# Cross-attention and a Fourier product on one core: a row left out of the first transform, 16-bit turning, a halved last product, one mask product

## What is computed

```python
x = x + xattn(layernorm(x), ctx, mask, wq, bq, wk, bk, wv, bv, wo, bo)   # x: 2 x 2048 x 512, ctx: 2 x 128 x 512
x = x + ffn(layernorm(x), w_freq_real, w_freq_imag, bias)

def xattn(...):   # 16 heads of 32
    score = einsum(q, k) / sqrt(32) * mask
    score = where(score == 0, -1e9, score)
    return softmax(score) @ v  @ wo + bo

def ffn(x, w_freq_real, w_freq_imag, bias):
    return real(ifft(fft(x) @ complex(w_freq_real, w_freq_imag))) + bias
```

## Time and profile before

| | |
|---|---|
| median of 3 runs | 470.81 (470.68 to 471.02) |
| the profiled execution's own time | 470.67 |
| its span, first to last instruction | 468.9 |
| granted TensorE clock, mean | 0.996 of full |
| TensorE busy | 449.5 (96%) |
| VectorE busy | 413.7 (88%) |
| ScalarE busy | 375.8 (80%) |
| GpSimd busy | 374.7 (80%) |
| chain that ended last | TensorE 70%, VectorE 12%, issue 7%, DMA 3%, GpSimd 3% |

### The profile page before, as it was taken

The page is one execution under the profiler, slowest core; times in us unless marked ns, Lnnn a source line. Parts: engine busy times, 40 slices in busy tenths (PEclk is TensorE's granted clock), DMA queues, the critical chain, the costliest instruction groups (busy, mean ns, idle before and its releaser), DMA issues.

```text
span 468.9 us, 11312 instructions
## 1 busy us (share of the span) xinstructions
PE 449.5 (96%) x3538; PEld 297.9 (64%) x3538; DVE 413.7 (88%) x698; ACT 375.8 (80%) x1431; POOL 374.7 (80%) x519
## 2 busy tenths in 40 slices
PE   7989979898999999999999999999999999999997
PEld 5877656676566666666666666666666666555443
DVE  4797499999999999999999999999999998999452
ACT  3358766789998989898989898988888898989620
POOL 6689666895998989898989898998989784866662
PEclk9999998999999999999999999999999999999999
DMA  8996834132435453644545554435332523331243
GB/s 291 396 358 166 263 137 112 42 86 69 93 82 133 114 141 107 141 120 125 136 114 146 100 121 117 108 105 143 105 95 62 98 75 80 78 92 25 67 112 113
DMA packets 83308, 59.37 MB, mean 127 GB/s; under 512 B 39729, under 2 KB 70705, under 8 KB 82738
## 3 DMA queue, kind: packets, MB, share of 16 engines
q1 hardware_dynamic: 82816, 58.55, 45.1%
q10 hardware_dynamic: 434, 0.10, 0.1%
HBM read 29.27 MB, written 8.39 MB: 80 GB/s over the span
## 4 chain that ended last, share of the span: by engine, by line
PE 70%; DVE 12%; issue 7%; DMA 3%; POOL 3%; SPq 2%; ACT 2%; DVEq 0%; POOLq 0%
PE bank L398 30%; PE bank L470 14%; PE bank L524 8%; PE bank L541 6%; PE bank L512 4%; DVE zs L786 3%; PE bank L537 2%; PE bank L403 2%; SPq L260 2%; DVE nmin L798 2%; DMA cxs<-in_ctx 1%; DMA xs<-in_x 1%; DVE zs L793 1%; PE bank L473 1%; ACT zs L626 1%
## 5 line engine op out<-in xcount | busy, mean ns | idle before, releaser
L626 ACT ACTIVATE zs<-zs,nbias 128x128 f32<-128x128 f32 x512 | 199.5, 397 | 5.4 <-POOL nbias L1018 5.2
L626 ACT ACTIVATION_READ_ACCUMULATOR zs<-zs,nbias 128x1 f32 x512 | 99.1, 194 | 0.0
L793 DVE SCALAR_TENSOR_TENSOR zs<-zs 128x1024 f32<-128x1024 f32 x64 | 92.0, 1437 | 2.3
L786 DVE TENSOR_TENSOR zs<-bank,ms 128x512 f32<-128x512 f32 x128 | 82.1, 683 | 0.0
L798 DVE TENSOR_REDUCE nmin<-zs 128x8 f32<-128x1024 f32 x64 | 77.2, 1206 | 0.1
L635 ACT COPY pt<-bank 128x512 f32<-128x512 f32 x128 | 68.5, 587 | 10.2 <-PE bank L524 9.7
L470 PE MATMUL bank<-xth,wqh 128*128 128x256 f16 x256 | 70.9, 277 | 2.2 <-DVE kl L745 1.8
L470 PE MATMUL bank<-xth,wql 128*128 128x256 f16 x256 | 70.4, 275 | 0.0
L470 PE MATMUL bank<-xtl,wqh 128*128 128x256 f16 x256 | 70.4, 275 | 0.0
L524 PE MATMUL bank<-ident,zs 128*128 128x128 f32 x512 | 67.0, 274 | 0.4 <-ACT zs L626 0.4
L1024 POOL COPY rzb<-rz 128x256 f32<-128x256 f32 x64 | 60.9, 951 | 3.1 <-DVE rz L803 2.2
(11 more groups left out here) (109 smaller groups left out, 983.9 us busy)
## 6 DMA issues: line engine op xcount, KB each, us to landing
xs<-in_x SPq DMA_DIRECT2D x16, 512.0 KB, 4.2
xtr<-in_xt SPq DMA_DIRECT2D x16, 512.0 KB, 4.7
out<-x SPq DMA_DIRECT2D x32, 256.0 KB, 2.3
qs<-qh SPq DMA_DIRECT2D x120, 64.0 KB, 2.0
lp<-in_lparts SPq DMA_DIRECT2D x4, 1024.0 KB, 9.2
qs<-ql SPq DMA_DIRECT2D x60, 64.0 KB, 2.0
ms<-in_mask SPq DMA_DIRECT2D x16, 128.0 KB, 2.3
wqs<-in_wq SPq DMA_DIRECT2D x2, 512.0 KB, 6.7
```

What stands on the lines that cost most here:

```text
L626: last = act.activation(z, z, ACT.Exp, bias=nbias[:, s % 4, i:i + 1], scale=-NEG, accum_out=zsum[:, s % 4, i:i + 1])
L786: dve.tensor_tensor(zs[:, s % NZ, t], A[n % 2][:].rearrange("p (h k) -> p h k", h=4), ms[:, c % NM, t, :].unsqueeze(1).broadcast_to([128, ...
L793: dve.scalar_tensor_tensor(out=z, in0=z, scalar=0.0, in1=z, op0=ALU.is_equal, op1=ALU.subtract).then_inc(eq_done, 1)
```

## The change

1. **Row of frequency 0.** In the host's table it is 0 in place of 0.5 for the first transform, so no mean has to be taken off: the statistics, their combination and the subtraction go from the four `U` fills. The second transform needs the 0.5: GpSimd writes it into the table in slot 8, once TensorE has done the last `U` fill, and the `M` fills wait for that.
2. **16-bit turning.** `stok` is float16, ScalarE makes a float16 copy of the identity in the head, and the turning is a plain float16 product against it.
3. **Halved last product.** The last `FF` fill becomes two, of columns 0 to 255 and 256 to 511, each with its own VectorE instruction and its own store.
4. **One mask product.** The two score banks are one tensor; a step has one mask product of 128x1024. It waits for both tiles' scores, and the next step's scores wait for all of it.

```diff
@@
+        if mid == [LAST]:
+            mid = [LAST, (*LAST, "right")]
@@
-        stok, _ = sb("stok", [128, 2, 2, 128], F32)
+        stok, _ = sb("stok", [128, 2, 2, 128], F16)
+        ident16, _ = sb("ident16", [128, 128], F16)
@@
-        bank = [stack.enter_context(nc.psum_tensor(f"bank{i}", [128, 512], F32)) for i in range(8)]
-        A, PB, CX, G = bank[0:2], bank[2:4], bank[4], bank[5:8]
+        A = stack.enter_context(nc.psum_tensor("scores", [128, 2, 512], F32))
+        bank = [stack.enter_context(nc.psum_tensor(f"bank{i}", [128, 512], F32)) for i in range(2, 8)]
+        PB, CX, G = bank[0:2], bank[2], bank[3:6]
@@
+
+        def columns(n):
+
+            if fills[n] == LAST:
+                return slice(0, 256)
+            return slice(256, 512) if fills[n][:3] == LAST else slice(0, 512)
@@
             def load_mask(c):
...
-                    sp.wait_ge(tt_done, 2 * (4 * (c - NM) + 3) + 2)
+                    sp.wait_ge(tt_done, 4 * (c - NM) + 4)
@@
             def store(c, t):
...
-                sp.wait_ge(g_free, at["FF", c, t] + 1)
-                sp.dma_start(o_d[:, n], x1[:, n % NO, :]).then_inc(d_o[n % NO], 16)
+                for f in fills:
+                    if f[:3] == ("FF", c, t):
+                        n1 = columns(at[f])
+                        sp.wait_ge(g_free, at[f] + 1)
+                        sp.dma_start(o_d[:, n, n1], x1[:, n % NO, n1]).then_inc(d_o[n % NO], 16)
@@
             def stat_rows(o, c):
...
+                if c == 0:
+                    pe.wait_ge(i16_done, 1)
...
-                    last = pe.transpose(o[:, 256 + 128 * t:384 + 128 * t], stok[:, c % 2, t], ident[:])
+                    last = pe.matmul(o[:, 256 + 128 * t:384 + 128 * t], stok[:, c % 2, t], ident16[:], start=True, stop=True)
@@
                 elif kind == "M":
...
+                    pe.wait_ge(dc_done, 1)
@@
-                    last = split_mm(o[:], [((h[:, f, k, :], l[:, f, k, :]), (mh[:, k, :], ml[:, k, :]))
-                                           for k in range(4)])
+                    n1 = columns(n)
+                    last = split_mm(o[:, n1], [((h[:, f, k, :], l[:, f, k, :]), (mh[:, k, n1], ml[:, k, n1]))
+                                               for k in range(4)])
...
             def scores(s, t):
...
-                if n >= 2:
-                    pe.wait_ge(tt_done, n - 1)
+                if t == 0 and s >= 1:
+                    pe.wait_ge(tt_done, s)
...
-                        last = full_mm(A[n % 2][:, 128 * j:128 * j + 128],
+                        last = full_mm(A[:, n % 2, 128 * j:128 * j + 128],
@@
+            act.wait_ge(d_eye, 16)
+            act.copy(ident16[:], ident[:]).then_inc(i16_done, 1)
@@
                 elif kind == "U":
...
-                    dve.bn_stats(stu[:], src[:, 0:256]).then_inc(u_done, 1)
-                    dve.wait_ge(u_done, 2 * c + 1)
-                    dve.bn_aggr(agu[:], stu[:]).then_inc(u_done, 1)
-                    dve.wait_ge(u_done, 2 * c + 2)
...
-                        last = dve.scalar_tensor_tensor(out=us[:, c, 256 * i:256 * i + 256], in0=src[:, 0:256],
-                                                        scalar=agu[:, 0:1], in1=od[:, c % 2], op0=ALU.subtract, op1=o)
+                        last = dve.tensor_tensor(us[:, c, 256 * i:256 * i + 256], src[:, 0:256], od[:, c % 2], o)
@@
                 elif kind == "FF":
...
-                    last = dve.scalar_tensor_tensor(out=x1[:, n1 % NO, :], in0=src[:], scalar=rs2[:, n1 % NO:n1 % NO + 1],
-                                                    in1=x1[:, n1 % NO, :], op0=ALU.mult, op1=ALU.add)
+                    z = x1[:, n1 % NO, columns(n)]
+                    last = dve.scalar_tensor_tensor(out=z, in0=src[:, columns(n)], scalar=rs2[:, n1 % NO:n1 % NO + 1],
+                                                    in1=z, op0=ALU.mult, op1=ALU.add)
@@
-            def mask_mul(s, t):
-                n = 2 * s + t
+            def mask_mul(s):
...
-                dve.wait_ge(sc_done, n + 1)
+                dve.wait_ge(sc_done, 2 * s + 2)
...
-                if t == 0 and s >= NZ:
+                if s >= NZ:
...
-                dve.tensor_tensor(zs[:, s % NZ, t], A[n % 2][:].rearrange("p (h k) -> p h k", h=4),
-                                  ms[:, c % NM, t, :].unsqueeze(1).broadcast_to([128, 4, KEYS]),
+                dve.tensor_tensor(zs[:, s % NZ], A[:].rearrange("p t (h k) -> p t h k", h=4),
+                                  ms[:, c % NM].unsqueeze(2).broadcast_to([128, 2, 4, KEYS]),
...
             def zero_to_neg(s):
...
-                dve.wait_ge(tt_done, 2 * s + 2)
+                dve.wait_ge(tt_done, s + 1)
@@
+
+            def constant_row():
+
+                pool.wait_ge(g_done, at["U", 3] + 1)
+                pool.memset(tb[0:1, 0, :], 0.5).then_inc(dc_done, 1)
@@
             for v in range(V0, V1):
...
+                if v == 8:
+                    constant_row()
@@
-    c[0] = 0.5
+    c[0] = 0.0```

On VectorE, slot 4 and the opening of slot 5 (`us` are the U fill's sums, `lp` the folding of the weights, `zs` the softmax tile, `nmin` its minimum). Before:

```order
L798 TENSOR_REDUCE nmin<-zs 128x8
L759 TENSOR_TENSOR ql<-bank,qh 128x256
L730 BN_STATS stu<-bank 128x6
L732 BN_AGGR agu<-stu 128x2
L735 SCALAR_TENSOR_TENSOR us<-bank,agu,od 128x256 x2
L823 BN_STATS st_91<-xs 128x6
L803 RECIPROCAL rz<-zsum 128x8
L828 BN_AGGR ag_92<-st_91 128x2
L841 TENSOR_TENSOR lp<-lp 128x512 x3
L786 TENSOR_TENSOR zs<-bank,ms 128x512 x2
L793 SCALAR_TENSOR_TENSOR zs<-zs 128x1024
```

More of the change, by code:

```diff
@@ L20 @@
 V0, V1 = 2, NS + 16
+LAST = ("FF", NC - 1, 1)
 NEG = 1e9
@@ L182, in build @@
         rs2, _ = sb("rs2", [128, NO], F32)
-        stu, _ = sb("stu", [128, 6], F32)
-        agu, _ = sb("agu", [128, 2], F32)
         nmin, _ = sb("nmin", [128, 4, 8], F32)
@@ L229, in build @@
         g_hi, ex_done, pt_copied, ch_done = (sem(n) for n in ("g_hi", "ex_done", "pt_copied", "ch_done"))
-        w_hi, w_sc, rc_done = sem("w_hi"), sem("w_sc"), sem("rc_done")
+        w_hi, w_sc, rc_done, i16_done = sem("w_hi"), sem("w_sc"), sem("rc_done"), sem("i16_done")
         h1_done, h2_done, st_done, wz_hi = (sem(n) for n in ("h1_done", "h2_done", "st_done", "wz_hi"))
@@ L235, in build @@
             sem(n) for n in ("rz_done", "cn_done", "s1_done", "a1_done", "s2_done", "a2_done", "w_lo"))
-        u_done, wz_lo, l0_done, m_hi, m_lo, b_zero, l2_done, l_hi, o_lo = (sem(n) for n in ("u_done", "wz_lo", "l0_done", "m_hi", "m_lo", "b_zero", "l2_done", "l_hi", "o_lo"))
+        dc_done, wz_lo, l0_done, m_hi, m_lo, b_zero, l2_done, l_hi, o_lo = (sem(n) for n in ("dc_done", "wz_lo", "l0_done", "m_hi", "m_lo", "b_zero", "l2_done", "l_hi", "o_lo"))
         p_l1, p_l2, p_zero = (sem(n) for n in ("p_l1", "p_l2", "p_zero"))
@@ L387, in _ @@
             for i in range(NO):
-                sp.wait_ge(d_o[i], 16 * len(range(i, 2 * NC, NO)))
+                sp.wait_ge(d_o[i], 16 * (len(range(i, 2 * NC, NO)) + (i == NO - 1)))
         @block.tensor
@@ L511, in scores @@
                 for j in range(4):
-                    last = pe.matmul(A[n % 2][:, 128 * j:128 * j + 128], qs[c % 2][0:96, g, j, 128 * t:128 * t + 128],
+                    last = pe.matmul(A[:, n % 2, 128 * j:128 * j + 128], qs[c % 2][0:96, g, j, 128 * t:128 * t + 128],
                                      ks[0:96, g, j, c // (NC // NB), :], start=True, stop=True)
@@ L892, in _ @@
             low_q(1)
-            mask_mul(0, 0)
-            mask_mul(0, 1)
+            mask_mul(0)
             lo(at["W1", 1])
@@ L899, in _ @@
             moments(2)
-            mask_mul(1, 0)
-            mask_mul(1, 1)
+            mask_mul(1)
             zero_to_neg(1)
@@ L916, in _ @@
                 if 0 <= v < NS:
-                    mask_mul(v, 0)
-                    mask_mul(v, 1)
+                    mask_mul(v)
                 if 0 <= v < NS:
@@ L1183, in dft_tables @@
     c, s = np.cos(2 * np.pi * kj / D), np.sin(2 * np.pi * kj / D)
-    c[0] = 0.5
+    c[0] = 0.0
     s[0] = 1.0 - 2.0 * (np.arange(n) % 2)
```

## The result

The changed kernel takes 467.07 us, the median of 4 runs (466.69 to 467.18), and the kernel before 470.78 beside it; the ratio is 0.9916, 95% interval 0.9904 to 0.9927. The forecast was 467.4, in a range of 465.2 to 468.9. The profiled execution took 467.02 us; its span is 465.2, 3.6 less than before, and its granted clock 1.0.

A forecast was written before the change was run, and what follows sets the result against it. VectorE was taken to bound from 56.48 to 87 us, TensorE from 129 to 386 and from 447 us. 1.75 + 1.07 + 0.3 + 0.25 = 3.4 us off 470.81 gave 467.4, 8 in 10 within 465.2 to 468.9.

The forecast's parts named there:

- U fills, 1.5 us at the point where TensorE takes over: VectorE, 57 to 87 us: four fills each lose 0.80 us, of which about 1.5 us reaches TensorE.
- the copy's end: GpSimd's copy of the reciprocals, slot 7: ends near 85.0 us, so TensorE's L537 behind it gains 1.0 us.
- the query's low part: Before TensorE's L470 at 87.42 us: a further wait for VectorE of 0.43 us goes as well.
- Something takes it back: Slots 5 and 7: VectorE and GpSimd stretch each other at the SBUF port, taking back part of the 3.2 us.
- the bound of 3.2 us: Upper bound for the four U fills' gain, 0.8 us each, if nothing is taken back.
- To 129 us 1.75: Early gain up to 129 us: U fills 1.5, sixth turning 0.1, two mask products 0.14 at 105 to 116 us.
- Ten turnings, 1.07: TensorE's long stretch: ten chunks' statistics turnings in 16 bits save 0.107 us each, 1.07 us.
- Tail masks 0.3: 393 to 434 us, eight VectorE slots: merged mask products save between 0 and 0.56 us; 0.3 taken.
- Constant row and identity 0: GpSimd's slot 8 memset costs 0 to 0.4 us, ScalarE's identity copy at most 0.37; both taken as 0.
- Halved last product 0.25: End of kernel: VectorE's last instruction loses 0.27 us, the smaller store saves 0; together 0.25 us.
- Rivals 1, 2 and 4: Port takes more, 468.6 (chance 0.14); all gain stays, 465.5 (0.13); merged product slow, 3.4 or 43 us lost (0.04).
- Rival 3: After 87 us, where TensorE bounds: a second stretch at 1.2 GHz loses 1.7 us, 469.1; chance 0.08.

The follow-up runs named there:

- part_last_product: The kernel before with only the last product halved, each half with its own store: 470.37 us, ratio 0.9985.
- third_U_fill_plain: The kernel before with only the third U fill (slot 6) without statistics and mean: 470.61 us, ratio 0.9992.
- the profile with one store: The kernel before with the halved last product but one whole 256 KB store at the end: 470.85 us against 470.83, ratio 0.9999.
- change_without_subtraction: The changed kernel with GpSimd subtracting only 8 of each 256 columns for chunk 4: 466.17 to 467.04 us, ratio 0.9911 to the kernel before.
- before_without_subtraction: The kernel before with GpSimd subtracting only 8 of each 256 columns for chunk 4: 470.32 us against 470.83, ratio 0.9989.

## Why the prediction was right, and where not

- **U fills, 1.5 us at the point where TensorE takes over:** 1.30 in one profile and 1.60 in the other. The fills of 0.66 us, the step of 1.52 us in slot 7, and the copy's end (forecast 85.0, 85.31 in the profile whose head is 0.24 late) came as written. By the prediction 1.0 of it hung on that copy and 0.43 on the query's low part; the experiments put it, head-relative, as 0.85 in the first profile and 1.14 in the second from an earlier start of the ring, and 0.45 within it (slot 7, by the turned order at the port). Of the ring's part 0.74 and 1.03 are there at L485 of slot 6 (78.35 and 77.89 against 78.85; forecast 0.88), and 0.11 is the turning that lies between, one of the five that I had saving nothing. That the result lies so near the forecast is in part luck: the kernel before's profile, from which both were read, has its stretch at 70.3 us and not at 75 to 79, where it would have been 0.6 us later at step 6. Against part_last_product's profile the same two gains are 1.9 and 2.2 us. The prediction priced a second stretch behind 87 us, and held that VectorE hides the one ahead of it; at 75.6 us it does not.
- **"Something takes it back":** this names only part of the reason why 3.2 us became 1.5. At the folding sums of slot 5 the port did take the fill's gain (3.87 us for 3.11). In slot 7 it holds 0.45, and without the subtraction the ring of slot 7 starts no earlier (80.89 against 80.85 us), because TensorE works without a pause from L485 of slot 6 to the scores of slot 7 and the ring follows from there. The gain of slot 6's fill on VectorE (its minimum came 2.60 us earlier in slot 7) ended as idle time before L772. So the bound of 3.2 us was out of reach by this order of work, not by the port alone.
- **To 129 us 1.75:** 2.1, head-relative, 0.11 of which is a turning that the prediction counts among the ten. Behind the U fills it had 0.24 (the sixth turning and two masks); the first profile has 0.10 at step 8, 0.25 more at step 10, and 0.46 more at step 12. The mask product's 0.14 was too small: alone it gained 0.35 between the turnings of steps 10 and 12. Five slots of 0.07 would be that; which ones was not separated. The 0.25 at step 10 is in no profile of the mask product or the 16-bit turning alone, but third_U_fill_plain has 0.21 there, so it goes with the U fills; how was not tried.
- **Ten turnings, 1.07:** nine lie between the turnings of steps 12 and 52, where 0.87 to 0.89 is gained in all three profiles, 0.10 for each; with the tenth, right ahead of step 12, it is 1.0. The four passes that the Trainium skill gives to true FP32 (FP8 and Floating Point Precision, "TensorE Precision Notes") would make it, by my estimate, three times that; the chain has half the time, no quarter. The instruction replaced is a transpose, but plain float32 products of this kernel show the same half: eight of 128x256 in a U fill take 1.73 us (82.79 to 84.52 in the kernel before), 0.216 each, and float16 products of 256 columns start 0.11 apart.
- **Tail masks 0.3:** 0.36 and 0.37, and 0.35 with the mask product alone. **Constant row and identity 0:** the memset took 0.30 us, and the groups list no wait for it; nothing else shows.
- **Halved last product 0.25:** 0.53. The step that failed is "256 KB land after 2.3 us and the masks' 128 KB after 2.3 too: 0". These medians are over the whole span and compare stores with loads; among the stores of the last 20 us 128 KB landed 0.3 us sooner than 256, and the profile with one store showed that it counts. Whether the loads or the other traffic made the medians alike was not separated.
- **Head 0:** 0.24 and 0.07 late. It differs from profile to profile, of kernels with the same head too: over all profiles chunk 4's statistics start between 55.80 and 57.55, always after a wait for the tokens' load.

Sum by the first profile: -0.24 + 1.30 + 0.80 + 0.89 + 0.36 + 0.53 = 3.64 us, for 3.4 forecast. The U fills and the turnings (as counted here) gave 0.2 less each, the stretch from 88 to 130 us 0.56 more, the last product 0.28 more, the tail 0.06 more, and the head, left out, cost 0.24. So the sum is nearer the forecast than its terms are. Rivals 1, 2 and 4 did not come about. Rival 3, a second stretch behind 87 us, did in one run of one part; it cost 1.28 us there, of which 0.9 stayed.

## What to carry to other kernels

When work leaves an engine that bounds one stretch, ask at which instruction the next engine takes over and follow the ring that feeds it: what lies on the freed engine behind that point becomes idle time, whatever the contention. A row that gives a time over the whole program (a DMA's median landing) is no price for the last one; read it in its own window, a store against stores. Where two engines share a port, moving an instruction moves its price to whatever it then lies beside; it must go to a place where the other engine does not use the port, and neither of the two places tried here was one. Before a gain is read off two profiles, see whether their stretches at the lower clock lie in the same places; a kernel that differs only behind the stretch in question shows how much that alone moves.

## What was new of the hardware

- A turned order at the SBUF port shows in short form: in change_without_subtraction a GpSimd subtraction of 32 columns takes 1.24 us behind VectorE's step of 1.51, and 0.27 us in before_without_subtraction, where no such step runs beside it. The Trainium skill calls the port a lock held for a whole instruction (SBUF — State Buffer, "SBUF: two separate sides"); the rows agree, and they add that a waiting instruction of the other engine came next.
- The stretches at 1.2 GHz in these profiles are all 3.4 us long and start at different places, in unchanged work too: at 70.3 us before, at 75.6, or at 62.4 and 76.1, in two kernels that differ from it only at the end, at 60.5 or nowhere with the change, and at 61.3, 74.9 and 115.9 with its first part. One at 75 to 79 us, just ahead of where TensorE takes over, moved step 6 by 0.6 us; one at 115.9 cost 1.28 us at once and 0.9 for good. The one at 75.6 follows an idle time of TensorE of 2.16 us, but the changed kernel has an idle time of 2.11 us at the same place (before 74.71) and no stretch. What brings one on was not tried.
- The stores of 128 KB in the last 20 us landed after 1.7 us, those of 256 KB after 2.0 (medians).
